# A graph network on one core: the stage that picks source rows by one-hot products handles its batches in pairs

## The reference

```python
deg_out = segment_sum(ones, row); deg_in = segment_sum(ones, col)
w = inv_sqrt(deg_out)[row] * inv_sqrt(deg_in)[col]
agg_fwd = segment_sum(w[:, None] * x[col], row)
agg_bwd = segment_sum(w[:, None] * x[row], col)
out = 0.5 * (agg_fwd @ W_src.T + b_src) + 0.5 * (agg_bwd @ W_dst.T + b_dst)
```

## Times and profile before

| what | value |
|---|---|
| median of 2 runs | 8533.69 us (8532.7 to 8534.68) |
| profiled execution, its own time | 8540.75 us |
| its span | 8538.9 us |
| PE busy | 6832.8 us, 80% |
| DVE busy | 6298.4 us, 74% |
| POOL busy | 4335.6 us, 51% |
| ACT busy | 3141.4 us, 37% |
| granted clock of PE, mean | 0.872 of full speed |

### The profile page before, as it was taken

The page is one execution under the profiler, slowest core; times in us unless marked ns, Lnnn a source line. Parts: engine busy times, 40 slices in busy tenths (PEclk is TensorE's granted clock), DMA queues, the critical chain, the costliest instruction groups (busy, mean ns, idle before and its releaser), DMA issues. The chain is left out here.

```text
span 8538.9 us, 219666 instructions
## 1 busy us (share of the span) xinstructions
PE 6832.8 (80%) x59894; PEld 5740.4 (67%) x60293; DVE 6298.4 (74%) x20368; ACT 3141.4 (37%) x8821; POOL 4335.6 (51%) x5493
## 2 busy tenths in 40 slices
PE   5865577789968888888886997884997884997887
PEld 4764466655556666666665777774996774897775
DVE  7999888832257777777776777776887776887777
ACT  3533322233323333333323551001660004668991
POOL 0000377400047777777752556774667771566770
PEclk8985689999977787878778999998999995999996
DMA  0000266510024444444433886777886763887772
GB/s 23 2 2 1 72 140 139 139 53 30 30 72 107 104 107 107 106 107 107 106 96 139 287 288 213 208 207 143 330 338 204 208 201 120 319 338 214 208 207 92
DMA packets 636888, 1262.19 MB, mean 148 GB/s; under 512 B 117598, under 2 KB 175621, under 8 KB 636385
## 3 DMA queue, kind: packets, MB, share of 16 engines
q1 hardware_dynamic: 415409, 704.46, 25.1%
q0 software_dynamic: 199040, 544.46, 23.6%
q10 hardware_dynamic: 22196, 10.20, 0.4%
HBM read 780.96 MB, written 477.75 MB: 147 GB/s over the span
## 5 line engine op out<-in xcount | busy, mean ns | idle before, releaser
L1177 POOL DMA_INDIRECT GS<-t1d,KI x1564 | 1486.8, 951 | 1293.8 <-POOLq L141 814.9
L1069 PE MATMUL PS<-w,AREA 128*128 128x128 f32 x6048 | 810.1, 283 | 158.8 <-DVE w L971 63.9
L1069 PE MATMUL PS<-w,GS 128*128 128x128 f32 x6128 | 796.4, 283 | 173.0 <-DVE AREA L1014 76.9
L1069 PEld LDWEIGHTS PS<-w,GS 128*128 128x128 f32 x6128 | 728.7, 193 | 241.0 <-DVE w L971 163.2
L1069 PEld LDWEIGHTS PS<-w,AREA 128*128 128x128 f32 x6048 | 722.4, 191 | 246.6 <-DVE w L971 137.5
L971 DVE TENSOR_TENSOR w<-PS,KI 128x512 f32<-128x512 f32 x964 | 666.8, 692 | 300.1 <-issue 283.4
L2484 PE MATMUL PS<-AREA 128*128 128x128 bf16 x13392 | 841.1, 219 | 20.9 <-ACT GS L2410 4.7
L2484 PEld LDWEIGHTS PS<-AREA 128*128 128x128 bf16 x13392 | 790.0, 98 | 77.1 <-POOL AREA L2428 9.1
L2459 DVE TENSOR_SCALAR AREA<-PS,w 128x1024 bf16<-128x1024 bf16 x558 | 716.0, 1284 | 156.8 <-PE PS L2470 78.5
L2428 POOL TENSOR_TENSOR AREA<-AREA,w 128x192 int32<-128x192 int32 x1116 | 529.5, 506 | 468.1 <-PE PS L2484 291.9
L2410 ACT ACTIVATE GS<-PS 128x1024 f32<-128x1024 f32 x558 | 571.7, 1025 | 310.5 <-PE PS L2484 298.9
(11 more groups left out here) (428 smaller groups left out, 14099.7 us busy)
## 6 DMA issues: line engine op xcount, KB each, us to landing
xbuf<-GS SPq DMA_DIRECT2D x558, 512.0 KB
XR<-in_edge_attr SPq DMA_DIRECT2D x780, 256.0 KB
pbuf<-AREA SPq DMA_DIRECT2D x482, 256.0 KB
GS<-t1d,KI POOLq DMA_INDIRECT x1564
AREA<-t2d ACTq DMA_DIRECT2D x121, 64.0 KB
GS<-xbuf,KI POOLq DMA_INDIRECT x484
keyd<-AREA POOLq DMA_INDIRECT x482
AREA<-xbuf,KI POOLq DMA_INDIRECT x480
```

The costliest lines, as they stand in the source:

```text
L1069: i = e.matmul(PS[:, s % 3, 0:128], feats(s)[0:m, r, 0:D], SELW[s % 3][0:m, width * r:width * r + 128], start=(r == 0), stop=(r == 3))
L1177: e.indirect_dma_start(GS[0:m, s, r, 0:wide], None, table, bass.IndirectOffsetOnAxis(ap=idx[0:m, c:c + 1].bitcast(U32), axis=0)).then_inc( ...
```

## The change

All edits are in `produce_p`. The batches are taken in 241 pairs, q = 0 to 240; a chunk is two pairs. The number of slots, UP, goes from 8 of one batch to 4 of a pair.

- One spread product serves a pair. Its moving operand holds the key rows of both batches on partitions 0 and 1 and constants on partitions 32 and 64, its weights are `SPW`, and each 32-bit word of the result holds the two keys, plus 128, as bf16 halves. One comparison with `IPB` (the partition's number plus 128) yields both one-hots.
- One row of `rowspd`, instead of two, is loaded for a chunk: two batches to each of two partitions.
- `picks` runs twice in a step, 24 products, with one signal `gm` at the end. The copy has 128x1024 elements, the store 512 KB.
- `load(ck + 2)` is issued behind the copy of the chunk's first pair (`s % 2 == 0`). PE's step q issues the spread of pair q + 2 ahead of the picks of pair q.
- Ahead of the loop VectorE clears 1024 columns in place of 2048, writes the constants and signals three times (`sw`).

```diff
+        NP2, UP = NBP // 2, 4
+        assert NBP % 2 == 0 and NBT >= 2
...
-        OHT = [area(256).bitcast(BF16) for _ in range(4)]
-        OUT = [area(512) for _ in range(UP)]
...
-        RWZ = area(2048)
-        RW = [RWZ[:, 1024 * i:1024 * i + 1024].bitcast(BF16).rearrange("o (j k) -> o j k", j=4) for i in range(2)]
+        OHT = [area(512).bitcast(BF16).rearrange("n (d k) -> n d k", d=2) for _ in range(4)]
+        OUT = [area(1024).rearrange("n (d k) -> n d k", d=2) for _ in range(UP)]
+        OHG, OUTG = OHT[0][:, 0, :], OUT[0][:, 0, :]
...
+        RWZ = area(1024)
+        RWB = RWZ.bitcast(BF16)
+        RW = [RWB[:, 1024 * i:1024 * i + 1024].rearrange("o (j k) -> o j k", j=2) for i in range(2)]
+        SPW = area(64).bitcast(BF16)
+        IPB, sw = area(1), p.sem("sw")
...
-        rv = rowspd.rearrange("d (c k) -> d c k", c=NCK)
+        pw = pbuf.rearrange("(q d p) k -> q p d k", d=2, p=128)
+        rv = rowspd[0].rearrange("(c q d k) -> c d q k", q=2, d=2, k=BE)
...
-                def step(b, s, it):
-                    e.wait_ge(ev, b + 1)
-                    e.dma_start(pv[bass.ds(b, 1)].rearrange("b p k -> (b p) k"), OUT[s]).then_inc(st[s], 16)
-                peeled(e, NBP, UP, step)
+                def step(q, s, it):
+                    e.wait_ge(ev, q + 1)
+                    e.dma_start(pw[bass.ds(q, 1)].rearrange("q p d k -> (q p) d k"), OUT[s]).then_inc(st[s], 16)
+                peeled(e, NP2, UP, step)
                 for s in range(UP):
-                    e.wait_ge(st[s], 16 * ((NBP - 1 - s) // UP + 1))
+                    e.wait_ge(st[s], 16 * ((NP2 - 1 - s) // UP + 1))
...
-                    past(e, gm, ck, 2, 4)
+                    past(e, gm, ck, 2, 2)
...
                 def load(ck, i):
                     lo = ranges(e, 1, ck * 8, 1)[0]
                     e.dma_start(TS[i], table[bass.ds(lo, 128), :]).then_inc(tl[i], 16)
-                    e.dma_start(RW[i][0:2].rearrange("o j k -> o (j k)"),
-                                rv[:, bass.ds(ck, 1), :].rearrange("d c k -> d (c k)")).then_inc(rl[i], 16)
+                    e.dma_start(RW[i][0:2], rv[bass.ds(ck, 1)].rearrange("c d q k -> (c d) q k")).then_inc(rl[i], 16)
                 e.wait_ge(k2, 4)
                 load(0, 0)
                 load(1, 1)
 
-                def step(b, s, it):
-                    e.wait_ge(gm, b + 1)
+                def step(q, s, it):
+                    e.wait_ge(gm, q + 1)
                     past(e, st[s], it, 1, 16)
-                    e.activation(OUT[s], PS[:, 4 + s % 4, :], ACT.Copy).then_inc(ev, 1)
-                    ck = it * 2 + s // 4
-                    if s % 4 == 1 and not (isinstance(ck, int) and ck + 2 >= NCK):
+                    e.activation(OUT[s], PS[:, 4 + 2 * (s % 2):6 + 2 * (s % 2), :], ACT.Copy).then_inc(ev, 1)
+                    ck = it * 2 + s // 2
+                    if s % 2 == 0 and not (isinstance(ck, int) and ck + 2 >= NCK):
                         e.wait_ge(tb, ck + 1)
-                        e.wait_ge(kb, b + 3)
-                        load(ck + 2, s // 4)
-                peeled(e, NBP, UP, step)
+                        e.wait_ge(kb, q + 2)
+                        load(ck + 2, s // 2)
+                peeled(e, NP2, UP, step)
...
+            for k in (32, 64):
+                e.memset(RWB[k:k + 1, :], 1.0)
+            e.memset(SPW, 0.0).then_inc(sw, 1)
+            e.wait_ge(sw, 1)
+            e.memset(SPW[32:33, :], 128.0)
+            e.memset(SPW[64:65, :], 67.0 / 256.0)
+            e.memset(SPW[0:2, :], 1.0).then_inc(sw, 1)
+            e.wait_ge(sw, 2)
+            e.memset(SPW[0:1, :], 2.0 ** -16)
+            e.tensor_scalar(IPB, IP[:], 128.0, None, ALU.add).then_inc(sw, 1)
+            e.wait_ge(sw, 3)
...
-                def step(b, s, it):
-                    e.wait_ge(kb, b + 1)
-                    past(e, gm, b, 4)
-                    e.tensor_scalar(OHT[s % 4], PS[:, s % 4, :], IP[:, 0:1], None, ALU.is_equal).then_inc(oh, 1)
-                peeled(e, NBP, UP, step)
+                def step(q, s, it):
+                    e.wait_ge(kb, q + 1)
+                    past(e, gm, q, 4)
+                    e.tensor_scalar(OHT[s], PS[:, s, :].bitcast(BF16).rearrange("n (k d) -> n d k", d=2),
+                                    IPB[:, 0:1], None, ALU.is_equal).then_inc(oh, 1)
+                peeled(e, NP2, UP, step)
...
-            def picks(q, i):
+            def picks(a, s, d, i):
                 for r in range(4):
                     for k in range(3):
-                        n = e.matmul(PS[:, 4 + q, 128 * r:128 * r + 128], OHT[q][:, 128 * r:128 * r + 128],
...
-                def spread(b, s, it):
-                    e.wait_ge(rl[s // 4], it * 16 + 16)
-                    past(e, oh, b, 4)
-                    e.matmul(PS[:, s % 4, :], K2, RW[s // 4][:, s % 4, :], start=True, stop=True).then_inc(kb, 1)
-
-                def step(b, s, it):
-                    if not (isinstance(b, int) and b >= NBP - 2):
-                        spread(b + 2, (s + 2) % UP, it + (s + 2) // UP)
-                    e.wait_ge(oh, b + 1)
-                    past(e, ev, b, 4)
-                    e.wait_ge(tb, it * 2 + s // 4 + 1)
-                    picks(s % 4, s // 4).then_inc(gm, 1)
+                def spread(q, s, it):
+                    e.wait_ge(rl[s // 2], it * 16 + 16)
+                    past(e, oh, q, 4)
+                    e.matmul(PS[:, s, :], SPW, RW[s // 2][:, s % 2, :], start=True, stop=True).then_inc(kb, 1)
+
+                def step(q, s, it):
+                    if not (isinstance(q, int) and q >= NP2 - 2):
+                        spread(q + 2, (s + 2) % UP, it + (s + 2) // UP)
+                    e.wait_ge(oh, q + 1)
+                    past(e, ev, q, 2)
+                    e.wait_ge(tb, it * 2 + s // 2 + 1)
+                    picks(4 + 2 * (s % 2), s, 0, s // 2)
+                    picks(5 + 2 * (s % 2), s, 1, s // 2).then_inc(gm, 1)
                 spread(0, 0, 0)
                 spread(1, 1, 0)
-                peeled(e, NBP, UP, step)
+                peeled(e, NP2, UP, step)
```

More of the change, by code:

```diff
@@ L2490, in produce_q @@
         p.run()
-    UP = 8
     def produce_p(table):
         p = Phase()
+        NP2, UP = NBP // 2, 4
+        assert NBP % 2 == 0 and NBT >= 2
         A0 = [0]
@@ L2571, in after @@
                     e.wait_ge(un, n)
-                    e.dma_start(pv[bass.ds(b, 1)].rearrange("b p k -> (b p) k"), OUT[0]).then_inc(gs, 16)
+                    e.dma_start(pv[bass.ds(b, 1)].rearrange("b p k -> (b p) k"), OUTG).then_inc(gs, 16)
                 e.nop().then_inc(gs, 16)
@@ L2654, in first @@
                     e.wait_ge(gs, b * 16 + 16)
-                    e.memset(OUT[0], 0.0).then_inc(bg, 1)
+                    e.memset(OUTG, 0.0).then_inc(bg, 1)
                     e.tensor_copy(PC, IP[:]).then_inc(pq, 1)
@@ L2662, in unit @@
                     e.wait_ge(pq, n + b)
-                    e.tensor_scalar(OHT[0], PS[:, 0, :], PC[:, 0:1], None, ALU.is_equal).then_inc(oh, 1)
+                    e.tensor_scalar(OHG, PS[:, 0, :], PC[:, 0:1], None, ALU.is_equal).then_inc(oh, 1)
                     e.wait_ge(oh, n)
@@ L2666, in unit @@
                     e.wait_ge(gm, n)
-                    e.tensor_tensor(OUT[0], OUT[0], PS[:, 4, :], ALU.add).then_inc(un, 1)
+                    e.tensor_tensor(OUTG, OUTG, PS[:, 4, :], ALU.add).then_inc(un, 1)
                     e.wait_ge(un, n + 1)
@@ L2674, in _ @@
             f = flag(e)
-            def picks(q, i):
+            def picks(a, s, d, i):
                 for r in range(4):
                     for k in range(3):
-                        n = e.matmul(PS[:, 4 + q, 128 * r:128 * r + 128], OHT[q][:, 128 * r:128 * r + 128],
+                        n = e.matmul(PS[:, a, 128 * r:128 * r + 128], OHT[s][:, d, 128 * r:128 * r + 128],
                                      TPC[i][:, k, :], start=(k == 0), stop=(k == 2))
@@ L2703, in unit @@
                     e.wait_ge(tb, n)
-                    picks(0, 0).then_inc(gm, 1)
+                    picks(4, 0, 0, 0).then_inc(gm, 1)
                 units(e, unit)
```

## The result

| what | before | after |
|---|---|---|
| median of the runs | 8533.69 us | 8711.56 us |
| profiled execution's span | 8538.9 us | 8709.4 us |
| ratio | | 1.021, 95% interval 1.0185 to 1.0234 |
| PE busy | 6832.8 us | 6817.8 us |
| mean granted clock of PE | 0.872 | 0.868 |

What follows compares the result with a forecast made beforehand. The prediction took the key rows' load, which PE's spread awaits once a chunk, as the bound: 119 x (6.2 - 3.91) = 273 us plus 1 on 8540.75 gives 8815, less 7 for the median, 8808 us; range 8690 to 8900.

Steps and rivals of the forecast that it cites:

- What binds, and why: In produce_p, PE's spread waits for key rows loaded two chunks ahead; about 2.4 us of standing still each chunk.
- the ring: Picks, copy, table load, key load, landing, spread and next picks, closing once for each chunk; 5.48 us at the upper clock.
- bound of +0.43 us: Addition to the 5.48 us if ScalarE's queue held the table load until the wider copy's end; kept as a bound.
- The -0.24 us for a shorter issue: Possible saving in the 5.48 us because the key load is smaller and its issue might take 245 ns, not 480.
- The standing still, 2.4 us: PE reaches the spread 1.3 us after the copy's start, key rows land at 3.73; about 2.4 us idle a chunk.
- a fixed 2.0 us: A DMA's size-independent cost, in place of 2.15 us for the key rows' landing; 5.33 us a chunk, 18 us less.
- The clock: PE's clock goes to and fro, half the chunks at each level; 6.2 us a chunk, mean granted clock near 0.7.
- the clock stays up: Rival: PE keeps the upper clock in this stage; 5.3 to 5.6 us a chunk, 187 us more, 8721 us; chance 0.18.
- My own case: Key rows bind in produce_p while the clock changes; 8808 us, alone spanning 8745 to 8870 us; chance 0.60.
- GpSimd's ring: Copy, table load, landing and GpSimd's split; 7.28 us for two chunks, far inside 12.4 us, so not binding.
- The 0.85 for a time over 2% above the kernel before: Whole kernel: chance 0.85 of slower by more than about 2%, 171 us; same 0.14, faster 0.01.
- The 96 us of the first paragraph: Gain in the stage if PE alone set the pace: 3.11 us a chunk, not 3.91, over 120 chunks.

Runs made afterwards that it cites:

- keys_second: The changed kernel with the key rows issued ahead of the table rows, behind the register load; 10190.65 us, 79 us above the kernel before, 4.64 us a chunk.
- look_one: The changed kernel with the spread issued one pair ahead, not two; 10131.91 us, 20 us above the kernel before; 4.19 us a chunk.
- deep_keys: The changed kernel with four key-row buffers, keys loaded four chunks ahead, table rows unchanged; 8535.32 us against 8529.01 for the kernel before, 3.90 us a chunk.
- single_late: The kernel before, single batches, with the load behind a chunk's fourth batch copy, not its second; 10279.77 us, 168 us above the kernel before.
- deep_both2: The changed kernel, in pairs, with four buffers for key and table rows, both loaded four chunks ahead; 8461.67 us, ratio 0.9923 to the kernel before.
- single_deep: The kernel before, single batches, with four buffers for key and table rows, loaded four chunks ahead; 8494.79 us, ratio 0.9957 to the kernel before.
- key_delay: The changed kernel with an extra, waited-for ScalarE copy between table load and key load; 8887.54 us, 6.79 us a chunk.
- load_later: The changed kernel with the load behind the copy of a chunk's second pair, not its first; 9228.64 us, 9.67 us a chunk.
- keys_first: The changed kernel with the key rows issued first in the load, ahead of the register load too; 10150.03 us, 39 us above the kernel before.
- store_waits: keys_first with SP storing even pairs only once the table rows have landed; 8617.34 us against 8527.09 for the kernel before, 4.68 us a chunk.
- keys_first_b: The same kernel as keys_first, run again in another session; 8580.14 us against 8532.0 for the kernel before, 4.29 us a chunk.

## Why the prediction was right, point by point

*What binds, and why.* The key rows, wanted by a spread that a lookahead of two steps puts a whole chunk ahead: shown. Two edits that shorten the ring in different ways (keys_second, look_one) give time back, more buffers (deep_keys) give back all of it, and the same distance between load and spread in single batches makes nearly the same loss (single_late, 168 us). Wide copies and stores are no loss by themselves (deep_both2 is 33 us faster than single_deep).

*The ring's length at the upper clock, 5.48 us.* The mean over the stage was 5.38 us by GpSimd's line. Term by term, forecast and then mean of the chunks: picks to copy 1.58 and 1.71, copy to table load 1.07 and 0.92, on to the key load 0.51 and 0.51, landing 2.15 and 1.93, spread to picks 0.17 and 0.30. The copy's greater length did not hold the queue up: the table load went out 0.97 and 0.79 us after the start of a copy of 1.02 us, so the bound of +0.43 us was not needed. The -0.24 us for a shorter issue did not come either; the key issue took 0.48 us as before.

*The standing still, 2.4 us.* The spread waited 1.94 us on average, since the key load went out 0.15 us sooner and landed 0.22 us sooner than I had it; the waits of 2.80 and 1.50 us above are the two cases. The prediction's other value for the landing, a fixed 2.0 us, was no floor here: in about half of the chunks the spread followed 1.47 to 1.71 us after the issue.

*The clock: this step was mis-sized.* I had half of the chunks at the lower level, 0.72 us a chunk. The granted clock was 0.95, the first pair's picks took over 2.4 us in 9 of 116 chunks, and the term shows only as the difference between 1.71 us and some 1.6 us from the picks to the copy, about 0.1 us. Of the 96 us between the forecast 8808 and 8711.56, that is some 70 us; the ring's own terms are the other 25. I had read the fall from a stretch with PE at 72% and a clock of 0.72, but that stretch runs other products with waits of another kind, and busy share alone did not carry over. What came out is the rival "the clock stays up", 8721 us, to which I had given 0.18. My own case alone spanned 8745 to 8870 us, and 8711.56 us lies outside it: the time is inside the range because the range took the rival in. That 8721 is so close has some luck in it, since a ring 0.2 us too long stood against a clock term of 0.1 us that it left out. The runs give three points for this stage: 61% busy at 0.95, 60% at 0.87 (key_delay), 53% at 0.70 (load_later), with 2.3, 3.3 and 4.8 us on average from the start of a chunk's last pick to that of the next chunk's first. Whether the share or the single pause's length decides is not told apart by them. The Trainium skill's page "TensorE: Matmul & The Clock Gate", section "HAM oscillation — how this bites in real kernels", has a kernel with a DMA wait of some 3 to 5 us in each tile that starts every tile at the lower clock. The prediction carried it over to a wait of 2.4 us, about which that kernel says nothing; the changed kernel does not behave so, and load_later, whose spreads wait 4.4 us on average, comes near it.

*The rest.* GpSimd's ring lay inside, as said (12.4 us were forecast for two chunks, it needed about 7). The chances had the sign right. The 0.85 for a time over 2% above the kernel before is neither borne out nor refuted: the median lies 2.1% above it, with 2% inside the interval.

*The win that was not there.* The 96 us of the first paragraph were PE's bound with nothing else binding; deep_both2, in which no load binds, came to 3.32 us a chunk where that bound says 3.11, and won 70 us. The prediction had compared ScalarE's copies with PE, 2.05 us against 3.11, and left out the issues that stand between them on the same engine; with them ScalarE needs 3.27 us, and PE's 3.11 us were out of reach.

## What to carry to other kernels

When an operation is made to serve two units of work, count each lookahead and each buffer again in units of work: a lookahead of two steps doubles, a prefetch distance of two chunks does not. For every load write down what must happen between its issue and its first use, and add the issue's own place in the queue; if the sum is longer than the work between, the loop runs at the load's latency, however little the engines have to do. Then look at what is issued just ahead of a small load: here the place of a 512 KB store mattered more than the size of the load. And count the DMA issues of an engine into its work: a copy behind them waits for them.

## What the runs showed of the hardware

- A key load of 4 KB was there for the spread 1.4 to 1.8 us after the start of its issue when it was issued just before, or up to 0.1 us behind, a store of 512 KB on another engine's queue (changed kernel, keys_second), and 2.0 to 2.6 us after it when it was issued 0.3 us behind the store. A table load of 64 KB took 2.0 us to GpSimd's start well clear of a store and 3.1 us less than 0.3 us behind one (deep_keys). In the changed kernel 0.17 us in the issue time (1.30 or 1.47 us after the copy's start, the store at 1.19) decides between the two, chunk by chunk. That the store's packets are what it waits for is inferred from these times and from keys_first and store_waits, not shown packet by packet.
- The register load and the table load's issue on ScalarE's queue ran on while its copy of 1.02 us was still at work (0.97 and 0.79 us after its start). The other way round it does not hold: the next copy started 0.10 us behind the end of the key load's issue, in every chunk of deep_both2.
- The same kernel took 8533 us in one session and 10111 us in another. This stage did not differ: look_one and keys_first took the same 4.19 and 4.3 us a chunk in both. The others did: behind the stage, keys_first needed 3878 us at 193 GB/s and keys_first_b 3375 us at 221 GB/s for the same work. Whether the chip makes the difference is open; the record gives chip number 4 for the 10111.45 us and for the 8527.09 us beside store_waits.
